# Expert tiles in pairs with the weights stationary, and another order of the work ahead of the experts

## The chip, the cores and the metric

The kernel runs on one core of one Trainium2 chip. The metric is the device time of one execution, from the runs' median. Engines are named PE (TensorE), ACT (ScalarE), DVE (VectorE), POOL (GpSimd) and SP (SyncE, which issues most of the DMA); each runs its own list of instructions in order, and they wait for one another through semaphores.

## The reference

The output is `x + attention(xn) + experts(xn)`, with `xn` the layer norm of `x` (2 x 1024 tokens of 512 values, fp32). Cut to what matters:

```python
# attention: 16 heads of 128 in 4 groups, causal, softmax, dense projection
# experts: sigmoid router with 8 groups of 4; the best 4 groups, then the best 6 of their experts
idx, w = _route(xf, Wr, br)                       # 6 of 32 experts for each of 2048 tokens
gate = zeros((T, E)).at[arange(T)[:, None], idx].add(w)
def step(acc, ew):
    w1, w2, g = ew                                # w1: 256 x 512, w2: 512 x 256
    h = square(relu(xf @ w1.T)) @ w2.T
    return (acc + g[:, None] * h, None)
shared = square(relu(x @ Ws1.T)) @ Ws2.T          # one shared expert, 512 wide
x + attn + shared + moe_out
```

## The kernel before

Every large product is made of three: an operand is split into an upper part that PE reads exactly (`_hi`, made by a copy on ACT) and the rest (`_lo`, subtracted on DVE), and hi x hi, hi x lo and lo x hi are summed in PSUM.

**Ahead of the experts.** 16 token tiles of 128 are loaded, normalised (`spread`, `normalize` on DVE, `root` on ACT, `normalize_last` on ACT), turned on PE (`turn_up`, 4 transposes), copied (`copy_up`), split (`upper_up`, `lower_up`) and multiplied with the router (`logits`, 8 fp32 products of 32 columns in the trace). The shared expert is 16 groups `hidden(j, m)` of 12 products of 512 columns, their relu, square and split on ACT and DVE (`relu_unit`, `square_unit`, `upper_unit`, `lower_unit`), and 16 groups `outputs(o, q)` of 12 products of 512 columns, added by DVE (`add_output`). From the logits DVE makes the routing, PE the ranks (`ranks`), and then DVE and ACT mark, token tile by token tile, which row of which expert's tile a token goes to (`mark_rows`: 6 `row_hot` of 128 columns, on ACT for odd tiles, and 6 `tile_hot` of MAXT columns), and PE sums the marks into a list of tokens (`list_rows`, 6 products of MAXT columns). `warm(n)` are products of ones that nobody reads. The order of all this on each engine is written out by hand, call by call.

**The experts.** An expert's tokens stand in tiles of 128 rows; `first_pair` holds where each expert's tiles begin, with at least 2 tiles for each. There are 111 tiles. POOL gathers the tokens of a tile by an indirect DMA into one of four slots (`xg`), four tiles ahead of PE. On PE a tile p is: `hidden_tile(p)`, 12 products of 256 columns with the tokens stationary (lines L861, L862, L865), in it the 4 transposes of the tokens of tile p+1 (L853); `output_tile(p-1)`, 6 products of 512 columns (L884, L885, L888); `transpose_hidden(p)`, 2 fp32 transposes (L897). In between ACT and DVE turn PSUM into operands: relu (L1242) on ACT, square (L1656) on DVE, transposed on PE, then `upper_hidden` (L1246, ACT) and `lower_hidden` (L1348, DVE); `upper_tokens` (L1231, ACT) and `lower_tokens` (DVE) do the same for the tokens; `copy_output` (L1252, ACT) takes the result of tile p-1 out of PSUM and SP stores it. ACT's order in a tile is relu(p), tokens(p+1), copy_output(p-1), upper_hidden(p).
An expert is its first tile, written out, and a loop over its others; four experts are written out in a loop of eight. Beside the first tile and behind the loop stand the four pieces of the weights of expert e+2: `upper_weights` (L1236, ACT, 512 columns) and `lower_weights` (DVE). They come by a 1 MB load of SP into one of two buffers (`eraw`), issued when the expert that had the buffer is lowered (`ew_lo`); the load for expert 2 (L472) waits for the four pieces of expert 0. The weights' slots alternate by pairs of experts between `wa_hi` and `w_hi`, so the names in the trace change every two experts.

**Behind them** comes attention, in eight groups, and the gathered sums of the experts' rows. `match_rows` reads what `y_filled` fills: the rows of `expert_outputs` above MINT tiles are filled with zeros by one DMA of ACT (L1180).

The named lines are those of the profile.

## Time and profile before

| | |
|---|---|
| median of 3 runs | 1529.18 us (1529.16 to 1531.23) |
| the profiled execution | 1530.99 us, its span 1529.2 us |
| mean granted clock of TensorE | 0.993 |
| PE, PEld, DVE, ACT, POOL busy | 99, 86, 74, 55, 19% of the span |
| chain of waits | PE 97%, DVE 2%, DMA 1% |
| ahead of the experts | 0 to 141.5 us |
| experts | 141.5 to 538.5 us |
| attention | 538.5 us to the end |

### The profile page before, as it was taken

To read this page: it belongs to the slowest core of one execution; us is meant where nothing else is said; L and a number is where in the kernel's file an instruction comes from. 1 tells how busy PE (TensorE), PEld (TensorE's weight loads), DVE (VectorE), ACT (ScalarE), POOL (GpSimd) and SP (SyncE) were. 2 spreads that over 40 slices of the span, in tenths; PEclk is the share of its full clock that TensorE was granted. 3 is DMA by queue.
4 is the path that set the end of the run, shared out by engine and by line. 5 is a ranking of instruction groups with operands and counts; after the bars stand their busy time and mean duration, and the time that the engine had idled before them with its cause. 6 is when DMAs were issued, how large, how long until landed. Compare 5 with 4: busy or idle time off the path is not lost.

```text
span 1529.2 us, 31143 instructions
## 1 busy us (share of the span) xinstructions
PE 1516.1 (99%) x8548; PEld 1308.5 (86%) x8549; DVE 1133.2 (74%) x2586; ACT 838.2 (55%) x1753; POOL 296.5 (19%) x540
## 2 busy tenths in 40 slices
PE   9999999999999999999999999999999999999998
PEld 7887888989888978888888888888888888888886
DVE  7887566666666669949948958966975994994896
ACT  5565666766766635535535634544553563553553
POOL 0002443444444301012002002102102101200211
PEclk8999999999999999999999999999999999999999
DMA  7875677777776712102102103412211210210111
GB/s 277 322 283 188 199 240 235 242 236 226 237 257 200 240 41 70 43 21 75 42 20 75 42 34 103 164 62 82 68 35 36 74 41 21 75 34 27 56 42 55
DMA packets 64774, 184.34 MB, mean 121 GB/s; under 512 B 7136, under 2 KB 7264, under 8 KB 60000
## 3 DMA queue, kind: packets, MB, share of 16 engines
q1 hardware_dynamic: 39888, 112.56, 20.9%
q0 software_dynamic: 16640, 54.54, 13.0%
q10 hardware_dynamic: 8208, 16.78, 2.8%
q8 instruction: 19, 0.31, 0.1%
q14 instruction: 19, 0.16, 0.0%
HBM read 123.29 MB, written 60.56 MB: 120 GB/s over the span
## 4 chain that ended last, share of the span: by engine, by line
PE 97%; DVE 2%; DMA 1%; ACT 0%; issue 0%; SPq 0%; DVEq 0%; ACTq 0%
PE bank L663 8%; PE bank L665 8%; PE bank L994 8%; PE bank L664 8%; PE ps_s L663 7%; PE ps_s L665 7%; PE ps_s L664 7%; PE ps_s L981 5%; PE ps_s L983 4%; PE ps_s L982 4%; PE ps_s L861 4%; PE ps_s L865 3%; PE ps_s L884 3%; PE ps_s L862 3%; PE ps_s L885 3%; PE ps_s L888 3%
## 5 line engine op out<-in xcount | busy, mean ns | idle before, releaser
L1323 ACT ACTIVATE probs<-probs,negmax 128x128 f32<-128x128 f32 (+7 forms) x256 | 197.4, 773 | 122.6 <-DVE negmax L1737 121.9
L1331 ACT ACTIVATE pT_hi<-bank 128x512 fp32r<-128x512 f32 x288 | 164.4, 595 | 143.6 <-PE bank L994 117.6
L1348 DVE TENSOR_TENSOR pT_lo<-bank,pT_hi 128x512 fp32r<-128x512 f32 x288 | 189.6, 684 | 41.1 <-ACT pT_hi L1331 40.1
L1737 DVE CUSTOM_DVE_ANT_0 probs<-ps_s,causal 128x128 f32<-128x128 f32 (+7 forms) x256 | 189.3, 752 | 17.2 <-PE ps_s L983 15.7
L427 POOL TENSOR_TENSOR settled<-ident 128x1 f32<-128x1 f32 x192 | 46.0, 239 | 789.0 <-DVE acc L1766 779.0
L994 PE MATMUL bank<-ident,probs 128*128 128x128 f32 x1152 | 157.0, 272 | 0.0
L994 PEld LDWEIGHTS bank<-ident,probs 128*128 128x128 f32 x1152 | 136.9, 141 | 19.8
L663 PE MATMUL ps_s<-xT_hi,wa_hi 128*128 128x512 f32 x384 | 152.7, 398 | 0.0
L665 PE MATMUL ps_s<-xT_hi,wa_lo 128*128 128x512 f32 x384 | 151.0, 393 | 0.0
L664 PE MATMUL ps_s<-xT_lo,wa_hi 128*128 128x512 f32 x384 | 150.3, 391 | 0.0
L1746 DVE TENSOR_SCALAR probs<-probs,rnorm 128x128 f32<-128x128 f32 (+7 forms) x256 | 133.4, 521 | 9.1
L981 PE MATMUL ps_s<-kT_hi,qT_hi 128*128 128x512 f32 (+5 forms) x384 | 134.0, 349 | 0.9 <-DVE qT_lo L1717 0.5
L983 PE MATMUL ps_s<-kT_hi,qT_lo 128*128 128x512 f32 (+5 forms) x384 | 131.2, 342 | 0.0
L982 PE MATMUL ps_s<-kT_lo,qT_hi 128*128 128x512 f32 (+5 forms) x384 | 130.9, 341 | 0.0
L663 PE MATMUL bank<-pT_hi,v_hi 128*128 128x512 f32 x288 | 123.6, 429 | 0.6 <-DVE cT_lo L1348 0.6
L1348 DVE TENSOR_TENSOR hT_lo<-ps_s,hT_hi 128x256 fp32r<-128x256 f32 x111 | 47.1, 424 | 93.6 <-ACT hT_hi L1246 91.9
L623 POOL DMA_INDIRECT xg<-normed_tokens,comb_idx x112 | 111.5, 995 | 24.0 <-issue 19.1
L665 PE MATMUL bank<-pT_hi,v_lo 128*128 128x512 f32 x288 | 113.5, 394 | 0.0
L1252 ACT ACTIVATE ysb<-ps_s 128x512 f32 x111 | 66.4, 598 | 85.6 <-PE ps_s L888 79.0
L664 PE MATMUL bank<-pT_lo,v_hi 128*128 128x512 f32 x288 | 112.7, 391 | 0.0
L652 POOL DMA_INDIRECT comb<-expert_outputs,comb_idx x96 | 105.1, 1095 | 19.7 <-issue 11.7
L663 PE MATMUL bank<-wa_hi,cT_hi 128*128 128x512 f32 x256 | 101.5, 396 | 1.4 <-DVE cT_lo L1348 1.4
(197 smaller groups left out, 3608.7 us busy)
## 6 DMA issues: line engine op xcount, KB each, us to landing
eraw<-we SPq DMA_DIRECT2D x37, 1024.0 KB, 7.4
expert_outputs<-ysb SPq DMA_DIRECT2D x111, 256.0 KB
araw<-wa SPq DMA_DIRECT2D x37, 512.0 KB, 3.8
expert_outputs<-comb ACTq DMA_DIRECT2D x1, 16384.0 KB, 44.2
normed_tokens<-xn SPq DMA_DIRECT2D x4, 1024.0 KB, 9.8
out<-acc SPq DMA_DIRECT2D x16, 256.0 KB, 2.6
acc<-x SPq DMA_DIRECT2D x2, 1024.0 KB, 13.7
turned_tokens<-xT_hi SPq DMA_DIRECT2D x2, 1024.0 KB, 6.3
```

The costliest lines, as they stand in the source:

```text
L663: pe.matmul(out_, lh, rh, start=(first and k == 0), stop=False)
L664: pe.matmul(out_, lh, rl, start=False, stop=False)
L665: mm = pe.matmul(out_, ll, rh, start=False, stop=(last and k == parts - 1))
L981: pe.matmul(o, q_h, kT_hi[:, ks], start=True, stop=False)
L982: pe.matmul(o, q_h, kT_lo[:, ks], start=False, stop=False)
L983: mm = pe.matmul(o, q_l, kT_hi[:, ks], start=False, stop=True)
L994: mm = pe.transpose(ps_t[blk % 2][:, h * P:(h + 1) * P], probs[:, i % 2, h, a * P:(a + 1) * P], ident[:, :])
L1323: act.activation(pr, pr, ACT.Exp, bias=negmax[:, i % 2, a:a + 1], scale=-1.0, accum_out=rowsum[:, i % 2, a:a + 1]).then_inc(exp_ready, 1)
L1331: act.activation(pT_hi[:, blk % RING, :], ps_t[blk % 2][:, :], ACT.Copy).then_inc(pt_hi_ready, 1)
L1348: dve.tensor_tensor(out_, whole, upper.bitcast(F32), ALU.subtract).then_inc(signal, 1)
L1737: dve.tensor_tensor_reduce(halves(probs[:, i % 2, a, 0:keys]), ps_s[:, s:s + parts, 0:keys // parts], halves(causal[:, SQ - keys:]), -1.0, ...
L1746: dve.tensor_scalar(pr, pr, rnorm[:, i % 2, a:a + 1], None, ALU.mult).then_inc(probs_ready, 1)
```

## The change

Five things change.

1. The first two tiles of every expert are a pair. Their tokens lie side by side (`xgT_hi`, `xgT_lo` get a dimension of 2), the weights are the stationary operand and the two tiles' 256 tokens the moving one (`hidden_pair`). The result is already turned, so there is no `transpose_hidden` for the two; ACT and DVE work on 128 x 256 for each m (`relu_pair`, `upper_pair` with Square on ACT, `square_pair`, `lower_pair` on DVE). `output_first` gives the first tile's result in a bank of its own (`ps_y2`), `output_tile` the second's in the turn behind.
2. An expert on PE is now `turn_tokens(lo+1)`, `output_tile(lo-1)` of the expert before, `hidden_pair`, `turn_tokens(lo+2)`, `output_first`, and the loop from the third tile on. `turn_tokens(q, bank)` is the choice of the slot and the 4 transposes that `hidden_tile` had inside.
3. The weight pieces stand in other places: 0 and 1 ahead of the pair's relu, 2 between m=0 and m=1, 3 behind `copy_output(lo)`.
4. Every expert has at least LEAST = 3 tiles, and MAXT follows a formula: 177 in place of 160.
5. The order written out ahead of the experts is another one on PE, ACT and DVE, with WARM 18 instead of 12. Up to the experts' loop the calls are the same but for one `warm(2)` fewer between the first logits. `lower_unit(6, 1)`, `add_output(2, 2)` and `add_output(2, 3)` move behind the copy of the list, and DVE waits for `room_free` before the first attention scores.

The core of the diff, the orders cut to what the prediction speaks of:

```diff
-MAXT = MINT + 2 * E
+LEAST = 3
+MAXT = max(LEAST * (E - n) + min(n * TILES, (T * TOPK + (P - 1) * n) // P) for n in range(E + 1))
...
-WARM = 12
+WARM = 18
...
             turn_up(0, 0)
+            warm(2)
             turn_up(0, 1)
-            warm(2)
             logits(0, 0)
-            warm(2)
             turn_up(0, 2)
+            logits(0, 1)
             turn_up(0, 3)
             warm(6)
-            logits(0, 1)
+            logits(0, 2)
             warm(2)
-            logits(0, 2)
             turn_up(0, 4)
             logits(0, 3)
             turn_up(0, 5)
+            turn_up(0, 6)
             logits(0, 4)
-            turn_up(0, 6)
             logits(0, 5)
             turn_up(0, 7)
+            hidden(0, 0)
             logits(0, 6)
-            hidden(0, 0)
             hidden(0, 1)
+            turn_up(1, 0)
+            logits(0, 7)
+            turn_up(1, 1)
             hidden(1, 0)
-            logits(0, 7)
-            turn_up(1, 0)
             hidden(1, 1)
-            turn_up(1, 1)
...
-            turn_up(1, 5)
-            logits(1, 2)
+            logits(1, 3)
             turn_up(1, 6)
             turn_up(1, 7)
-            logits(1, 3)
             logits(1, 4)
             logits(1, 5)
             logits(1, 6)
             logits(1, 7)
+            hidden(4, 0)
             outputs(0, 0)
+            hidden(4, 1)
             outputs(0, 1)
-            hidden(4, 0)
+            hidden(5, 0)
+            ranks()
+            hidden(5, 1)
             outputs(0, 2)
             outputs(0, 3)
-            ranks()
-            hidden(4, 1)
+            hidden(6, 0)
+            list_rows(0)
+            hidden(6, 1)
+            list_rows(1)
...
             outputs(2, 2)
-            list_rows(13)
-            outputs(2, 3)
             list_rows(14)
             list_rows(15)
+            outputs(2, 3)
             outputs(3, 0)
             outputs(3, 1)
             outputs(3, 2)
...
+        ps_x2 = banks[0][:, :]
+        ps_p = [bank[:, 0:2 * P] for bank in banks[1::2]]
+        ps_y2 = banks[2][:, :]
...
+            def hidden_pair(lo, s):
+
+                w_hi, w_lo = w1(hi_slot(s)), w1(lo_slot(s))
+                both = lambda x, k: x[:, k, :, :].rearrange("p t n -> p (t n)")
+                for m in range(KM):
+                    ms = slice(m * P, (m + 1) * P)
+                    if m == 0:
+                        pe.wait_ge(mx_hi, lo + 2)
+                    for k in range(KD):
+                        pe.matmul(ps_p[m], w_hi[:, k, ms], both(xgT_hi, k), start=(k == 0), stop=False)
+                        pe.matmul(ps_p[m], w_lo[:, k, ms], both(xgT_hi, k), start=False, stop=False)
+                    if m == 0:
+                        pe.wait_ge(mx_lo, lo + 2)
+                    for k in range(KD):
+                        mm = pe.matmul(ps_p[m], w_hi[:, k, ms], both(xgT_lo, k), start=False, stop=(k == KD - 1))
+                    mm.then_inc(mh_ready, 1)
+
+            def output_first(lo, s):
+
+                w_hi, w_lo = w2(hi_slot(s)), w2(lo_slot(s))
+                for m in range(KM):
+                    pe.wait_ge(mhhi_ready, past(lo + (m + 1)))
+                    pe.matmul(ps_y2, hT_hi[:, m, 0, :], w_hi[:, m, :], start=(m == 0), stop=False)
+                    pe.matmul(ps_y2, hT_hi[:, m, 0, :], w_lo[:, m, :], start=False, stop=False)
+                    pe.wait_ge(mhlo_ready, past(lo + (m + 1)))
+                    mm = pe.matmul(ps_y2, hT_lo[:, m, 0, :], w_hi[:, m, :], start=False, stop=(m == KM - 1))
+                mm.then_inc(my_ready, 1)
...
             def expert_tiles(e, s, lo, hi, es):
 
-                pe.wait_ge(ew_lo, (e + NSH) * WP + 2)
-                hidden_tile(lo, slot_of(s))
-                after = pair_bound(pe, e + 2)
+                turn_tokens(lo + 1, ps_x2)
                 if s:
                     output_tile(lo - 1, slot_of(s - 1))
                 else:
                     with pe.If(es > 0):
                         output_tile(lo - 1, slot_of(SLOTS - 1))
-                transpose_hidden(lo, (e + (NSH + 1)) * WP)
-                with pe.Fori(lo + 1, hi) as p:
+                after = pair_bound(pe, e + 2)
+                pe.wait_ge(ew_lo, (e + NSH) * WP + 2)
+                hidden_pair(lo, slot_of(s))
+                pe.sem_inc(mt_ready, 2)
+                turn_tokens(lo + 2, ps_x)
+                pe.wait_ge(ew_lo, (e + (NSH + 1)) * WP)
+                output_first(lo, slot_of(s))
+                with pe.Fori(lo + 2, hi) as p:
                     hidden_tile(p, slot_of(s))
                     output_tile(p - 1, slot_of(s))
                     transpose_hidden(p)
...
+            def relu_pair(lo, m):
+
+                act.wait_ge(mh_ready, lo + (m + 1))
+                act.wait_ge(mhsq_ready, past(lo))
+                act.activation(prelu[:, m, :], ps_p[m], ACT.Relu).then_inc(mrelu_ready, 1)
+
+            def upper_pair(lo, m):
+
+                act.wait_ge(mrelu_ready, past(lo + (m + 1)))
+                act.activation(hT_hi[:, m, :, :].rearrange("p t n -> p (t n)"), prelu[:, m, :],
+                               ACT.Square).then_inc(mhhi_ready, 1)
+
...
             def expert_uppers(e, s, lo, hi, es):
 
                 arrived, slot = e // 2 + (NSH // 2 + 2), slot_of(s + 2)
-                relu_hidden(lo)
-                upper_tokens(lo + 1)
+                upper_tokens(lo + 1, 1)
                 upper_weights(0, slot, arrived)
                 if s:
                     copy_output(lo - 1)
                 else:
                     with act.If(es > 0):
                         copy_output(lo - 1)
-                upper_hidden(lo)
                 after = pair_bound(act, e + 2)
                 upper_weights(1, slot, arrived)
-                with act.Fori(lo + 1, hi) as p:
+                relu_pair(lo, 0)
+                upper_pair(lo, 0)
+                upper_weights(2, slot, arrived)
+                relu_pair(lo, 1)
+                upper_pair(lo, 1)
+                upper_tokens(lo + 2)
+                copy_output(lo, ps_y2)
+                upper_weights(3, slot, arrived)
+                with act.Fori(lo + 2, hi) as p:
                     relu_hidden(p)
                     upper_tokens(p + 1)
                     copy_output(p - 1)
                     upper_hidden(p)
-                upper_weights(2, slot, arrived)
-                upper_weights(3, slot, arrived)
...
+            def square_pair(lo, m):
+
+                dve.wait_ge(mrelu_ready, past(lo + (m + 1)))
+                dve.tensor_tensor(phsq[:, m, :], prelu[:, m, :], prelu[:, m, :], ALU.mult).then_inc(mhsq_ready, 1)
+
+            def lower_pair(lo, m):
+
+                dve.wait_ge(mhhi_ready, past(lo + (m + 1)))
+                dve.wait_ge(mhsq_ready, past(lo + (m + 1)))
+                subtract(hT_lo[:, m, :, :].rearrange("p t n -> p (t n)"), phsq[:, m, :],
+                         hT_hi[:, m, :, :].rearrange("p t n -> p (t n)"), mhlo_ready)
...
             spread(0)
+            spread(1)
             normalize(0)
-            spread(1)
             normalize(1)
             spread(2)
             lower_up(0, 0)
+            lower_up(0, 1)
             normalize(2)
-            lower_up(0, 1)
             lower_up(0, 2)
             lower_shared(0, 0, 1)
+            lower_up(0, 3)
             lower_shared(0, 1, 2)
+            spread(3)
...
             dve.wait_ge(started, 4)
+            lower_unit(6, 1)
+            add_output(2, 2)
+            add_output(2, 3)
             lower_unit(7, 0)
             lower_unit(7, 1)
-            add_output(2, 3)
+            lower_weights(0, 0, slot_of(0))
+            lower_weights(0, 1, slot_of(0))
             add_output(3, 0)
-            lower_weights(0, 0, slot_of(0))
             add_output(3, 1)
+            lower_weights(0, 2, slot_of(0))
             add_output(3, 2)
-            lower_weights(0, 1, slot_of(0))
-            lower_weights(0, 2, slot_of(0))
-            lower_weights(0, 3, slot_of(0))
             lower_tokens(0)
             add_output(3, 3)
+            lower_weights(0, 3, slot_of(0))
             for c in range(WP):
                 lower_weights(1, c, slot_of(1))
...
             def expert_lowers(e, s, lo, hi, es):
                 slot = slot_of(s + 2)
-                square_hidden(lo)
-                lower_tokens(lo + 1)
+                lower_tokens(lo + 1, 1)
                 lower_weights(e + 2, 0, slot)
-                lower_hidden(lo)
                 after = pair_bound(dve, e + 2)
                 lower_weights(e + 2, 1, slot)
-                with dve.Fori(lo + 1, hi) as p:
+                square_pair(lo, 0)
+                lower_pair(lo, 0)
+                lower_weights(e + 2, 2, slot)
+                square_pair(lo, 1)
+                lower_pair(lo, 1)
+                lower_tokens(lo + 2)
+                lower_weights(e + 2, 3, slot)
+                with dve.Fori(lo + 2, hi) as p:
                     square_hidden(p)
                     lower_tokens(p + 1)
                     lower_hidden(p)
-                lower_weights(e + 2, 2, slot)
-                lower_weights(e + 2, 3, slot)
```

## Rows read from the trace of the kernel before

**Rows 1.** Busy time by stage: stretch; busy us of each engine; PEclk; DMA share; GB/s.
```profile
17.00:27.00 10.00, 10.00 (x44) 9.42 (x43) 9.85 (x27) 3.96 (x8) 0.00 (x0) 0.50 1.04 390
58.00:65.00 7.00, 7.00 (x23) 5.89 (x23) 4.60 (x11) 3.61 (x7) 0.00 (x0) 0.52 1.00 402
146.00:150.00 4.00, 4.00 (x19) 3.61 (x19) 2.74 (x5) 2.39 (x5) 0.94 (x4) 0.59 1.00 406
175.13:535.70 360.57, 360.57 (x2449) 323.81 (x2448) 225.36 (x426) 245.06 (x528) 144.55 (x297) 1.00 0.73 233
```

**Rows 2.** Timeline, start of the kernel: start us, us, engine, line, what, [idle before].
```profile
14.96 1.92 DVE L1398 TENSOR_SCALAR xn<-res,mv,rstd 128x512 f32<-128x512 f32 x4
...
24.16 0.77 PE L663 MATMUL ps_s<-xT_hi,w_hi 128*128 128x512 f32 x1
...
33.91 0.97 PE L700 MATMUL bank<-wr_sb,xf 128*128 128x32 f32 x8
```

**Rows 3.** Timeline of PE, an expert of three tiles, its last tile in parts.
```profile
256.74 0.36 PE L861 MATMUL ps_s<-wa_hi,xgT_hi 128*128 128x256 f32 x1
...
263.89 0.36 PE L861 MATMUL ps_s<-wa_hi,xgT_hi 128*128 128x256 f32 x1
...
265.41 0.60 PE L853 MATMUL ps_s<-ident,xg 128*128 128x128 f32 x4
265.77 0.48 PE L884 MATMUL ps_s<-wa_hi,hT_hi 128*128 128x512 f32 x1
...
267.24 0.38 PE L897 MATMUL ps_s<-ident,mhsq 128*128 128x128 f32 x2
267.38 0.36 PE L861 MATMUL ps_s<-w_hi,xgT_hi 128*128 128x256 f32 x1
```

**Rows 4.** Timeline of PE, end of the last tile of the last expert.
```profile
535.70 0.38 PE L897 MATMUL ps_s<-ident,mhsq 128*128 128x128 f32 x2
536.96 0.50 PE L884 MATMUL ps_s<-w_hi,hT_hi 128*128 128x512 f32 x1 [0.88 <-ACT hT_hi L1246]
...
538.46 0.40 PE L663 MATMUL ps_s<-xT_hi,wa_hi 128*128 128x512 f32 x1
```

**Rows 5.** Timeline of ACT, the same place.
```profile
536.03 0.60 ACT L1252 ACTIVATE ysb<-ps_s 128x512 f32 x1 [0.93 <-PE ps_s L888]
536.53 0.38 ACT L1246 ACTIVATE hT_hi<-ps_s 128x256 fp32r<-128x256 f32 x1
```

**Rows 6.** Timeline of all engines, from the end of a hidden product group to the square.
```profile
194.65 0.60 PE L853 MATMUL ps_s<-ident,xg 128*128 128x128 f32 x4
194.85 0.38 ACT L1242 ACTIVATE mrelu<-ps_s 128x256 f32<-128x256 f32 x1 [0.64 <-PE ps_s L865]
...
195.27 0.43 DVE L1656 TENSOR_TENSOR mhsq<-mrelu 128x256 f32<-128x256 f32 x1 [0.59 <-ACT mrelu L1242]
```

**Rows 7.** Timelines of SP, PE, DVE and ACT, the first expert.
```profile
141.01 0.33 SPq L472 DMA_DIRECT2D eraw<-we  x1
...
141.47 0.28 PE L861 MATMUL ps_s<-wa_hi,xgT_hi 128*128 128x256 f32 x1
...
142.28 2.49 DVE L1348 TENSOR_TENSOR wa_lo<-eraw,wa_hi 128x512 fp32r<-128x512 f32 x4
...
145.16 0.44 PE L897 MATMUL ps_s<-ident,mhsq 128*128 128x128 f32 x2 [1.67 <-DVE mhsq L1656]
...
145.89 0.63 ACT L1236 ACTIVATE w_hi<-eraw 128x512 fp32r<-128x512 f32 x1 [1.77 <-DMA eraw<-we]
...
157.36 0.38 PE L897 MATMUL ps_s<-ident,mhsq 128*128 128x128 f32 x2
```

**Rows 8.** Timelines of PE and DVE, the ranks and the marks.
```profile
78.17 2.22 PE L751 MATMUL bank<-rsel,ones 128*128 128x480 f32 x15
...
94.92 1.07 DVE L1525 TENSOR_SCALAR row_hot<-lane,xf 128x128 f16<-128x128 f16 x6 [2.63 <-PE bank L761]
...
125.86 1.46 DVE L1527 TENSOR_SCALAR tile_hot<-lane,xf,tok_f 128x160 f16<-128x160 f16 x6
```

More of the change, by code:

```diff
@@ L883, in output_tile, with transpose_hidden @@
                 for m in range(KM):
-                    pe.matmul(ps_y, hT_hi[:, m, :], w_hi[:, m, :], start=(m == 0), stop=False)
-                    pe.matmul(ps_y, hT_hi[:, m, :], w_lo[:, m, :], start=False, stop=False)
+                    pe.matmul(ps_y, hT_hi[:, m, 1, :], w_hi[:, m, :], start=(m == 0), stop=False)
+                    pe.matmul(ps_y, hT_hi[:, m, 1, :], w_lo[:, m, :], start=False, stop=False)
                 pe.wait_ge(mhlo_ready, past(p + 1))
                 for m in range(KM):
-                    mm = pe.matmul(ps_y, hT_lo[:, m, :], w_hi[:, m, :], start=False, stop=(m == KM - 1))
+                    mm = pe.matmul(ps_y, hT_lo[:, m, 1, :], w_hi[:, m, :], start=False, stop=(m == KM - 1))
                 mm.then_inc(my_ready, 1)
-            def transpose_hidden(p, weights=None):
+            def transpose_hidden(p):
                 pe.wait_ge(mhsq_ready, past(p + 1))
                 for m in range(KM):
-                    if m and weights is not None:
-                        pe.wait_ge(ew_lo, weights)
                     mm = pe.transpose(ps_g[:, m * P:(m + 1) * P], mhsq[:, m * P:(m + 1) * P], ident[:, :])
@@ L1143, in _ @@
             square_unit(0, 0)
             relu_unit(0, 1)
+            copy_up(1, 0)
+            upper_up(0, 7)
             upper_unit(0, 0)
-            root(4)
+            relu_unit(1, 0)
+            copy_up(1, 1)
+            relu_unit(1, 1)
+            exponent(0)
+            upper_up(1, 0)
+            copy_up(1, 2)
+            upper_up(1, 1)
+            copy_up(1, 3)
+            upper_up(1, 2)
+            normalize_last()
             square_unit(0, 1)
+            relu_unit(2, 0)
@@ L1646, in _, with lower_tokens @@
             dve.wait_ge(hot_used, TILES)
             dve.tensor_copy(tok_idx[:, 0:MAXT], ps_list).then_inc(list_ready, 1)
-            def lower_tokens(q):
+            def lower_tokens(q, second=0):
                 dve.wait_ge(mx_hi, q + 1)
-                subtract(xgT_lo[:, :, :], ps_x.rearrange("p (k n) -> p k n", k=KD), xgT_hi[:, :, :], mx_lo)
+                subtract(xgT_lo[:, :, second, :], (ps_x, ps_x2)[second].rearrange("p (k n) -> p k n", k=KD),
+                         xgT_hi[:, :, second, :], mx_lo)
@@ L1731, in attend_dve @@
                             dve.wait_ge(pt_ready, n * TRI + blocks_before(i - 1))
+                        if isinstance(n, int) and n == 0 and unit == 0:
+                            dve.wait_ge(room_free, 1)
                         s = 2 * (unit % 2)
```

279 lines of the change are left out of this document (132 added, 147 removed).

## The prediction

> **What bounds the kernel now.** I read the chain of waits first: nearly all of it is PE. Then busy time by stage: in the expert stage PE is busy for all of 360.57 us, at the full granted clock [rows 1]. So only time on PE's own line counts, or a wait that opens in it. Ahead of the experts PE is also back to back from 16 us on, but two stretches run at the lower of its two levels (1.2 instead of 2.4 GHz): 17 to 27 us and 58 to 65 us [rows 1]. Each has fp32 logits and transposes ahead of it; the first shared-expert product starts at 24.16 [rows 2]. The attention stage behind the experts (538.46 on) is the same in both kernels but for one wait, dealt with below.
>
> **Steady expert tile.** In the timeline of PE a tile is: 12 products of 256 columns, 263.89 to 265.41 (1.52 us); 4 transposes of the next tokens to 265.77 (0.36); 6 products of 512 columns to 267.24 (1.47); 2 transposes of the hidden values to 267.38 (0.14); in all 3.49. The four products at 264.93 take 0.48, so 12 of them are 1.43, and the 0.09 over that is a slow restart behind fp32 transposes. An expert of three tiles takes 10.64 (256.74 to 267.38, where the weights' name changes) [rows 3]. There are 111 tiles; by the changes of name and the tile starts no expert has fewer than three, so the new least of 3 (it was 2) pads nothing.
>
> **The pair: what goes.** hidden_pair has the same 24 products of 256 columns as two tiles had: 24 x 0.119 = 2.85 us. What goes is transpose_hidden for both, with the slow restart behind it, 2 x (0.14 + 0.09) = 0.46, and the 0.15 by which an expert's first tile is now longer than its others (10.64 - 3 x 3.49). Saved per expert: 0.6 us, 19 us over 31 experts, if no wait opens.
>
> **The pair: the wait that it opens.** Now a tile's hidden transposes are followed by the next tile's 12 products and 4 transposes (1.87 us), and these cover the trip over ACT before output_tile. In the change an expert begins with turn_tokens(lo+1) and then at once output_tile(lo-1). The trace shows this trip without cover once, behind the last tile: transposes at 535.70, the output products at 536.96, with 0.88 us idle [rows 4]. ACT's rows say why: the copy of the output before it starts at 536.03, and only behind it, at 536.53, hT_hi [rows 5]. That order stays. Of the 1.26 us the transposes (0.13) and turn_tokens (0.35 + 0.05 of restart) cover 0.53, so each of 31 seams has a new PE wait of 0.73 us.
> The rest of such an expert, from T, the start of the last hidden transposes: output_tile from T+1.26, 1.50 long (536.96 to 538.46) to 2.76; the pair to 5.61; turn_tokens(lo+2) to 5.96; output_first. Its last product wants mhlo for m=1: PE's end at 5.61 + 0.20 to ACT's relu (194.65 to 194.85), + 0.42 to DVE (195.27) [rows 6] = 6.23; but DVE first lowers weight piece 2 (0.60 each: four of them from 142.28, 2.49 with the tail of the last [rows 7]), whose upper half, 0.63 long behind relu and Square of m=0, leaves ACT at 5.7, so the square starts near 6.3, the subtract at 6.8 and PE has it at 7.3; it wants it at 7.21. Wait: 0.1. Then output_first ends at 7.53, hidden_tile 1.43 to 8.96, turn 0.35, output_tile 1.47: the next T is at 10.78. Against 10.64 that is **+0.14 us for an expert of three tiles**, and the same for those of four and five, since a tile of the inner loop stays 3.49. 31 x 0.14 = +4.3. Bounds for one expert: -0.6 (the trip fully covered) to +0.5 (PE's register load, which now stands between output_tile and the pair with little queued ahead of it, costs up to 0.4; now it has backlog and no row shows it). I take +0.14, since both of its ends are rows of the same operations. The sem_inc of mt_ready is an instruction of PE's queue alone and hides in the products' backlog. ACT's and DVE's other work is the same but for the copies and squares of 2 x 256 columns; the weight loads of DMA are asked for at T+3.6 of the expert before, about 8.7 us ahead of use, and one took 4.9.
> The gathers of POOL keep four slots and four tiles of lead. The wait of DVE on room_free before the first attention scores costs nothing: the last store goes out near 540 and the scores come 8 projections of 2.8 us later.
>
> **The first expert.** The load for expert 2 is issued when lower_weights(0,3) is done, now 141.01, and lands for ACT at 145.89, 4.9 later [rows 7]. PE ends the stage before at E = 141.47. In the change lower_weights(0,3) stands behind add_output(3,3), which waits for PE's end: done at E+1.5, landed at E+6.4. And ACT has upper_weights(0) of that load ahead of relu_pair(0), so the relu starts at E+7.5 and output_first at E+8.4 (relu 0.42, square and subtract 0.42 each, as in [rows 6]), where PE stood ready at E+6.8, having waited 2.4 us before that for mx_lo behind four lower_weights on DVE (E+4.5). The first two tiles are done at E+10.75, two more take 6.7 to the last hidden transposes: E+17.5. With one more stretch at the lower clock behind these gaps (+1.0 on what is not waiting) E+18.5, against E+15.9 before (157.36) [rows 7]: **+2.6**, bounds 0 and +5.
>
> **The other order ahead of the experts.** spread(1) before normalize(0) puts the first transposes 1.3 later; 18 warm products instead of 12 fill just that. Tokens 4 to 7 are normalised at 14.2 instead of 14.96 [rows 2]: 0.75 earlier. logits(0,6) goes behind hidden(0,0), out of the slow stretch: twice 0.81 there, 0.81 at the full clock (33.91 to 34.72) [rows 2]. With PE's last gap before these transposes gone too, hidden(0,0) starts at 21.1 instead of 24.16, about 2.3 of it real. In the second slow stretch ten us of nothing but logits and transposes preceded the outputs; now two of the eight logits, two turns and two products stand apart and some 5 us are left in a row, so I take the stretch of 7 us, worth 3.4, as gone. Ranks end at 74.7 instead of 80.25 (78.17 + 2.1) [rows 8]: -5.5. From there to E are 61.2 us now. In them DVE's marks pace the lists: it waits 2.6 us for PE once (94.92), which the new order, with lists put in earlier, spares; but MAXT goes from 160 to 177, and six tile_hot take 1.46 with the tail of the last, 0.23 each [rows 8], so 96 of them with 17 columns more cost between 0 and 96 x 0.025 = 2.4, and I take 1.7. The last list then comes 6.4 earlier than now, and behind it PE has one output group more than it has now, 2.9, and half a us of restarts. So E = 74.7 + 61.2 - 2.6 + 1.7 + 3.4 = 138.4: **-3.1**, bounds -6.5 (DVE never late) and 0 (the second slow stretch stays, 3.4 less the 0.3 above). The fill of expert_outputs grows from 16.8 to 21.2 MB, from 44 to 56 us; it ends near 115, ahead of its first reader.
>
> **The sum.** -3.1 + 2.6 + 4.3 = +3.8 us. The profiled execution took 1530.99 (span 1529.22 and 1.8 around it), so 1534.8 on its scale; the median of the runs is 1.8 lower, 1529.18, so **1533.0**. From no change a measurement can tell about 0.2%, 3.06 us: the limits are 1526.1 and 1532.2.
>
> **Clock between the gaps.** Behind the last tile 0.88 us idle did not lower the clock: the six products of 512 columns behind it take 1.50 [rows 4], as at full clock (1.47 in [rows 3]). At the first expert 1.67 us of idle up to 145.16 [rows 7] was followed by a lower clock: 0.59 in the mean from 146 to 150 [rows 1], 3.4 us at the lower level. The Trainium skill, page "TensorE: Matmul & The Clock Gate", section "A second HAM failure mode: psum-queue depth-cycling", tells of short idles between groups of products that recur often enough for the clock to swing between its levels. That speaks against this change, which makes 31 such idles; by the one row at hand they are too short.
>
> **The rivals.**
> 1. The seam is covered and the pair pays: 31 x -0.64 = -19.8, with -3.1 and +2.6: -20.3, 1508.9. For it: PE's work itself is 10.0 us for three tiles. Against it: [rows 4, 5]. This is the case on the other side; it decides as soon as hT_hi is ready less than 0.5 us behind the transposes.
> 2. Nothing net: the seam costs what the transposes gave (0 per expert) and the first expert's wait is half of mine: -3.1 + 1.3 = -1.8, 1527.4. For it: +0.14 is the difference of two sums of 10 us.
> 3. The recurring gaps lower the clock, once per expert 3.4 us at half speed: 31 x 1.7 = +53, 1586. For it: it happened after 145. Against: [rows 4].
> 4. The order ahead brings nothing, since the slow stretch stays or DVE's marks come late: +2.6 + 4.3 = +6.9, 1536.1.
>
> **How the numbers follow.** Forecast 0.48, rival 1 0.13, rival 2 0.18, rival 3 0.06, rival 4 0.15. The forecast's own range is 1529 to 1540; about 0.15 of its 0.48 is under 1532.2. Faster: rival 1 and 0.07 of rival 2, 0.20. Same: 0.15 of the forecast, 0.11 of rival 2 and 0.01 of rival 4, 0.27. Slower: 0.53. The range of 8 in 10 leaves out rivals 1 and 3 and reaches down to half a covered seam (31 x 0.35 less, 1521) and up to 0.4 more in a third of the experts on top of rival 4: 1520 to 1543.
>
> **What would show it.** PE idle before the output products (now L884) with ACT's hT_hi as releaser, 31 times, 0.7 us; three-tile experts of 10.8; first expert 18.5 us from the last shared output to the transposes of its last tile; the first shared-expert product at 21; full clock at 58 to 65; the last list near 123; the shared stage's end near 138. I am wrong if the three-tile expert is 10.3 or less, if the granted clock in the expert stage is below 1.00, or if the stage ahead ends behind 141.

## The result, and the profile after

The changed kernel takes 1540.99 us (median of 4 runs, 1539.26 to 1541.67) against 1529.20 (4 runs, 1529.16 to 1531.23): 1.0086 times as long, 95% interval 1.0063 to 1.0109. By the medians it is slower by 11.8 us, where 3.8 were predicted. The profiled execution took 1539.26 us, its span is 1537.5.

Three marks on PE's timeline cut each span into four parts: up to E, the start of the next tokens' transposes or products behind the last shared output; the first expert, from E to T, the start of its last hidden transposes; the other 31 experts, to the T of the last; and the rest. A seam is the place where one expert's last tile meets the next expert's first. Each ratio is to runs of before that were taken with the experiment (medians 1530.87 for e1 to e4, 1530.44 for e5 to e8, 1530.38 for e9 to e12), so it differs a little from a quotient with 1529.20.

| kernel | median us (runs) | ratio to before, 95% interval | E | first expert | 31 experts | rest of the span |
|---|---|---|---|---|---|---|
| before | 1529.20 (4) | | 141.47 | 15.89 | 378.34 | 993.5 |
| changed | 1540.99 (4) | 1.0086 (1.0063 to 1.0109) | 134.34 | 18.85 | 393.56 | 990.8 |
| e1 order alone | 1525.43 (12) | 0.9976 (0.9959 to 0.9993) | 134.45 | 16.61 | 378.46 | 993.1 |
| e2 pair alone | 1543.93 (5) | 1.0103 (1.0069 to 1.0137) | 142.01 | 16.22 | 393.64 | 990.3 |
| e3 piece 2 later | 1532.37 (12) | 1.0023 (1.0004 to 1.0041) | 134.56 | 18.92 | 386.75 | 990.3 |
| e4 seam | 1534.06 (12) | 1.0041 (1.0022 to 1.0060) | 135.64 | 19.23 | 387.12 | 990.3 |
| e5 160 columns | 1542.77 (4) | 1.0076 (1.0062 to 1.0091) | 135.57 | 19.10 | 393.54 | 993.4 |
| e6 before, 18 warm | 1529.42 (12) | 0.9988 (0.9972 to 1.0003) | 139.92 | 14.51 | 377.83 | 993.1 |
| e7 both mends | 1521.60 (5) | 0.9941 (0.9928 to 0.9954) | 137.71 | 17.54 | 376.27 | 990.1 |
| e8 and first expert | 1518.29 (5) | 0.9925 (0.9911 to 0.9938) | 134.71 | 15.70 | 376.29 | 989.8 |
| e9 changed, 12 warm | 1540.52 (6) | 1.0096 (1.0061 to 1.0131) | 136.10 | 18.18 | 393.75 | 990.5 |
| e10 layout | 1518.12 (8) | 0.9936 (0.9911 to 0.9960) | 134.01 | 15.79 | 376.12 | 990.1 |
| e11 wide | 1526.21 (10) | 0.9979 (0.9960 to 0.9997) | 136.75 | 15.75 | 376.17 | 996.0 |
| e12 old order, mends | 1525.60 (12) | 0.9966 (0.9948 to 0.9985) | 142.25 | 15.39 | 376.29 | 990.1 |

For the change: -7.1 + 3.0 + 15.2 - 2.7 = +8.3 us of span. The other 3.5 us of the 11.8 are scatter: the profiled execution of before is 1.8 above its median, that of the changed kernel 1.7 below, and before's 29 runs beside e1 to e4 went from 1521.0 to 1534.1.

Busy time by stage, of the changed kernel (the columns of [rows 1]: stretch; us, PE, PEld, DVE, ACT, POOL; PEclk; DMA share; GB/s):
```profile
17.00:27.00 10.00, 10.00 (x68) 8.92 (x67) 9.54 (x24) 5.48 (x11) 0.00 (x0) 1.00 1.04 396
58.00:65.00 7.00, 7.00 (x32) 5.68 (x31) 6.40 (x64) 1.12 (x2) 0.00 (x0) 1.00 1.00 371
140.00:147.00 7.00, 6.38 (x24) 4.99 (x24) 4.11 (x8) 4.24 (x10) 1.91 (x3) 0.51 0.94 372
153.19:546.75 393.56, 382.28 (x2445) 323.16 (x2444) 234.45 (x446) 269.70 (x552) 157.15 (x312) 1.00 0.70 224
```
Both slow stretches ahead of the experts are gone, where [rows 1] had 0.50 and 0.52, and the first one behind E is longer. In the 31 experts PE, never idle in [rows 1], is idle for 11.3 us, 5.4 of them ahead of the seams' output products, 4.9 ahead of the transposes of tokens that an expert now begins with, and 0.9 inside output_first; the clock stays at 1.00.

The timeline of PE, one expert of three tiles (start us, duration, line, what; to be held against [rows 3]):
```profile
304.07 0.38 PE L930 MATMUL ps_s<-ident,mhsq 128*128 128x128 f32 x2
304.48 0.65 PE L858 MATMUL bank<-ident,xg 128*128 128x128 f32 x4
305.33 0.50 PE L920 MATMUL ps_s<-wa_hi,hT_hi 128*128 128x512 f32 x1 [0.21 <-issue]
...
306.84 0.28 PE L883 MATMUL bank<-xgT_hi,wa_hi 128*128 128x256 f32 x1
...
309.72 0.60 PE L858 MATMUL ps_s<-ident,xg 128*128 128x128 f32 x4
310.08 0.48 PE L896 MATMUL bank<-wa_hi,hT_hi 128*128 128x512 f32 x1
...
311.59 0.51 PE L899 MATMUL bank<-wa_hi,hT_lo 128*128 128x512 f32 x1
311.93 0.28 PE L907 MATMUL ps_s<-wa_hi,xgT_hi 128*128 128x256 f32 x1
...
315.20 0.38 PE L930 MATMUL ps_s<-ident,mhsq 128*128 128x128 f32 x2
```
The expert takes 11.13. From the hidden transposes to the output product are 1.26, as at the tail of [rows 4]; the mean over 31 seams is 1.28. The profile puts this wait down to hT_hi at some seams and to no releaser ("issue") at others; here ACT's hT_hi ends at 305.28, 0.05 ahead of the product. The pair takes 2.88. The six products of output_first, 310.08 to 311.93, take 1.85, where 1.57 was predicted.

ACT, then DVE, beside that output_first:
```profile
307.84 0.63 ACT L1274 ACTIVATE w_hi<-eraw 128x512 fp32r<-128x512 f32 x1
...
309.22 0.62 ACT L1274 ACTIVATE w_hi<-eraw 128x512 fp32r<-128x512 f32 x1
309.92 0.39 ACT L1286 ACTIVATE prelu<-bank 128x256 f32<-128x256 f32 x1
```
```profile
308.50 0.69 DVE L1402 TENSOR_TENSOR w_lo<-eraw,w_hi 128x512 fp32r<-128x512 f32 x1 [1.41 <-ACT w_hi L1274]
309.11 0.42 DVE L1709 TENSOR_TENSOR phsq<-prelu 128x256 f32<-128x256 f32 x1
309.63 0.43 DVE L1402 TENSOR_TENSOR hT_lo<-phsq,hT_hi 128x256 fp32r<-128x256 f32 x1
309.98 0.69 DVE L1402 TENSOR_TENSOR w_lo<-eraw,w_hi 128x512 fp32r<-128x512 f32 x1
310.58 0.42 DVE L1709 TENSOR_TENSOR phsq<-prelu 128x256 f32<-128x256 f32 x1
311.10 0.43 DVE L1402 TENSOR_TENSOR hT_lo<-phsq,hT_hi 128x256 fp32r<-128x256 f32 x1
```
DVE waits last at 308.50. From there to the second hT_lo it goes from one operation to the next, weight piece 2 (309.98) among them, and PE's last product starts 0.49 behind the start of that hT_lo.

The first expert, to be held against [rows 7], and the tail:
```profile
134.34 0.60 PE L858 MATMUL bank<-ident,xg 128*128 128x128 f32 x4
135.62 0.39 PE L883 MATMUL bank<-xgT_hi,wa_hi 128*128 128x256 f32 x1 [0.69 <-ACT xgT_hi L1268]
...
138.89 0.74 PE L888 MATMUL bank<-xgT_lo,wa_hi 128*128 128x256 f32 x4 [2.05 <-DVE xgT_lo L1402]
...
143.12 0.76 PE L896 MATMUL bank<-wa_hi,hT_hi 128*128 128x512 f32 x1 [0.62 <-DVE w_lo L1402]
...
153.19 0.38 PE L930 MATMUL ps_s<-ident,mhsq 128*128 128x128 f32 x2
...
546.75 0.38 PE L930 MATMUL ps_s<-ident,mhsq 128*128 128x128 f32 x2
548.01 0.50 PE L920 MATMUL ps_s<-w_hi,hT_hi 128*128 128x512 f32 x1 [0.89 <-ACT hT_hi L1296]
```
Three waits of PE stand behind E; the tail's wait is that of [rows 4].

### The profile page after: what moved, and what is told of

It is laid out like the page before. It is cut to its first block, busy times and chain, and to the rows that moved or that the text cites. A ratio compares the mean times of both kernels' runs of the same rounds, so it can differ in the third digit from the quotient of the medians.

```text
span 1537.5 us, 30805 instructions
## 1 busy us (share of the span) xinstructions
PE 1512.3 (98%) x8424; PEld 1286.4 (84%) x8425; DVE 1132.4 (74%) x2586; ACT 851.2 (55%) x1753; POOL 302.6 (20%) x540
## 4 chain that ended last, share of the span: by engine, by line
PE 84%; issue 7%; DVE 5%; ACT 1%; POOL 1%; ACTq 1%; DMA 1%; DVEq 0%; POOLq 0%; SPq 0%
PE bank L669 7%; PE bank L1031 7%; PE bank L671 7%; PE bank L670 7%; PE ps_s L669 6%; PE ps_s L671 6%; PE ps_s L670 6%; PE ps_s L1018 4%; PE ps_s L1020 4%; PE ps_s L1019 4%; PE ps_s L920 3%; PE ps_s L924 2%; PE ps_s L921 2%; PE ps_s L858 2%; PE ps_s L911 1%
## 5 line engine op out<-in xcount | busy, mean ns | idle before, releaser
L433 POOL TENSOR_TENSOR settled<-ident 128x1 f32<-128x1 f32 x192 | 49.3, 257 | 786.5 <-DVE acc L1839 776.5
L629 POOL DMA_INDIRECT xg<-normed_tokens,comb_idx x112 | 117.5, 1049 | 23.8 <-issue 18.6
L671 PE MATMUL bank<-wa_hi,cT_lo 128*128 128x512 f32 x256 | 100.0, 391 | 0.0
L670 PE MATMUL bank<-wa_lo,cT_hi 128*128 128x512 f32 x256 | 99.7, 390 | 0.0
```

The lines of the kernel that those rows point to most:

```text
L670: pe.matmul(out_, lh, rl, start=False, stop=False)
L671: mm = pe.matmul(out_, ll, rh, start=False, stop=(last and k == parts - 1))
```

## The experiments

**e1: the order ahead of the experts and 18 warm products, in the kernel before.** The four blocks of PE, ACT and DVE are the changed kernel's; the experts are the old ones.

> The kernel before with one part of the change: the order ahead of the experts on PE, ACT and DVE and 18 warm products; the experts, their least of 2 and the 160 columns of the lists as before. Theory A (the traces of before and after are the sum of three terms: order -7.1, first expert +3.0, seams 31 x 0.49 = +15.2): the stage ahead ends near 134.3, and the old first expert is late only by the load that is now asked for behind it, 0 to +1.5: 1522.1 to 1523.6. Theory B (the order was sized right in the prediction, -3.1, and 4 us of the gap between the profiles is chance): 1526 to 1527.5. Theory C (an earlier end only makes the first expert wait for its weights, and all is given back there): 1528 to 1530.

Measured 0.9976, -3.7 us (-6.3 to -1.1); the medians differ by 5.4. E is 134.45, the first expert takes 0.7 longer than before, the rest is as before. Theory A by the trace. But the runs say more. With the mean granted clock at 1.000 the kernel before takes 1521.0 and 1521.7 us, at 0.997 1524.2, at 0.992 and 0.993 (15 of 29 runs) 1530.9 and more; the order alone takes 1523.8 to 1527.9 at 1.000 to 0.996. So its gain is a clock that stays up, and at the same clock it is some 2.5 us slower. Most of that is the first expert: 16.61 at a clock of 1.00 here, with 2.26 us of idle ahead of its first hidden transposes, against 14.51 at 1.00 and 1.67 in e6, which has the old order. The windows of e1:
```profile
17.00:27.00 10.00, 10.00 (x68) 8.93 (x66) 9.25 (x23) 5.74 (x12) 0.00 (x0) 1.00 1.04 392
58.00:65.00 7.00, 7.00 (x32) 5.68 (x31) 6.41 (x62) 1.12 (x2) 0.00 (x0) 1.00 0.98 348
```

**e2: the pair alone.** The changed kernel with the old order and 12 warm products.

> The changed kernel with the old order ahead of the experts and 12 warm products: the pair alone, with lists of 177 columns. Theory A: +15.2 from the seams and 0 to +3 from the first expert (the load for expert 2 is asked for ahead of the last output group again, so that part of its delay goes; the four lowerings of weights ahead of the first pair's marks stay): +15 to +18, 1544 to 1547. Theory B (the pair costs +4.3 + 2.6 as predicted and the rest of the +11.8 lies in how the new order and the pair meet): 1535 to 1537.

Measured 1.0103, +15.8 us (+10.6 to +21.0): theory A. The 31 experts take 393.64, as in the changed kernel, so nothing in them comes from the order. The first expert loses only 0.3 (at a clock of 0.89 in both; at 1.00 it is 15.39 in e12 against 14.51 in e6, 0.9). So most of its 3.0 in the changed kernel is the two parts' meeting.

**e3: weight piece 2 later**, on ACT and DVE:
```
-    lower_weights(e + 2, 2, slot)
     square_pair(lo, 1)
     lower_pair(lo, 1)
     lower_tokens(lo + 2)
+    lower_weights(e + 2, 2, slot)
```

> The changed kernel with weight piece 2 cast on ACT and lowered on DVE behind the next tokens instead of ahead of the second half of the pair. Theory A (output_first is late by 0.37 because DVE runs back to back from weight piece 1 to the lower part of hidden half 1): output_first falls from 1.84 to 1.5 and the kernel gains up to 31 x 0.35 = 11 us, 1530; less whatever the next tokens or the output copy now wait for. Theory B (output_first is late by the round trip of the second half itself, 0.2 + 0.42 + 0.42 + 0.42 behind its last product): the gain is under 31 x 0.1 = 3 us, 1538 to 1541. Rival: the weights come too late and tile 2 waits: slower than 1541.

Measured 1.0023 against the changed kernel's 1.0086: 9.6 us by the ratios, 8.6 by the medians, 6.8 of them in the 31 experts. Output_first fell from 1.83 to 1.61 in the mean of 30. Theory A in kind; 0.22 per expert, not 0.35, since two waits of 0.2 stay, for the second half's hT_hi and for its hT_lo. What PE's weight loads waited for (us in total, times, longest), the changed kernel from 160 to 540, then e3 from 160 to 520:
```profile
PEld bank L899 <- DVE hT_lo L1402: 13.8, 30, 0.5
PEld bank L896 <- ACT hT_hi L1291: 6.7, 30, 0.2
```
```profile
PEld bank L899 <- DVE hT_lo L1402: 7.0, 29, 0.2
PEld bank L896 <- ACT hT_hi L1291: 6.6, 29, 0.2
```
The wait for the second half's hT_lo falls from 0.46 to 0.24 each time; the one for its hT_hi stays at 0.2.

**e4: the seam.** The last output_tile of an expert goes to the other bank, and in ACT's loop
```
-    copy_output(p - 1)
     upper_hidden(p)
+    copy_output(p - 1)
```
with a wait for that copy ahead of the inner tiles' output products.

> The changed kernel with the last output_tile of an expert written to the other output bank, so that ACT can do upper_hidden of a tile ahead of the copy of the output before it. Theory A (the trip of 1.29 at the seam is ACT's copy of 0.5 plus upper_hidden): the seam's wait falls from 0.77 to between 0.3 and 0.5, 31 x 0.3 = 9 us and the same at the tail once, 1532; inner tiles stay at 3.48. Theory B (the seam is bound by PE's own sequencer, the loop's exit and the turn's start, and the copy hides behind it): 0 to 3 us, 1538 to 1541. Rival: the later copy makes output_first or DVE's store wait, and what the seam gains is given back there: 1541.

Measured 1.0041, 6.9 us less than the changed kernel, 6.4 in the 31 experts. The trip from hidden transposes to output product fell from 1.28 to 0.98, and at the tail from 1.26 to 0.85. But output_first grew to 1.97. PE and ACT at one seam:
```profile
303.21 0.38 PE L932 MATMUL ps_s<-ident,mhsq 128*128 128x128 f32 x2
303.63 0.65 PE L858 MATMUL bank<-ident,xg 128*128 128x128 f32 x4
304.06 0.49 PE L922 MATMUL bank<-wa_hi,hT_hi 128*128 128x512 f32 x1
```
```profile
303.63 0.39 ACT L1298 ACTIVATE hT_hi<-ps_s 128x256 fp32r<-128x256 f32 x1 [1.01 <-issue]
303.91 0.59 ACT L1304 ACTIVATE ysb<-ps_s 128x512 f32 x1
```
The upper half is now first on ACT, and the turn of tokens (0.43) covers what is left of it. Theory A; 0.3 x 31, some 9.5 us, gained, 0.14 x 31 = 4.3 given back in output_first, and 0.02 less in each of output_tile and the pair. At 24 of the 31 seams the trip is now 0.85 to 0.96; at the other seven it is 1.21 to 1.44, of which more in e7.

**e5: lists and buffer of 160 columns**, MAXT = MINT + 2 * E.

> The changed kernel with lists of 160 columns instead of 177 (MAXT = MINT + 2 E), so that the buffer of expert outputs and its fill are as large as before; nothing else. Theory A (17 more columns cost nothing behind the new order, since the marks are ahead of PE, and the attention stage is 2.7 us shorter in all kernels with the pair for another reason, such as where the loop's code lies): 1540 to 1541 and 990.3 us from the last hidden transposes to the end. Theory B (the larger buffer is what changed the attention stage, 990.3 us instead of 993.3): it is back at 993.3, 1543. Theory C (DVE's marks paced the stage ahead as the prediction had it, 1.7 us): 1539 and a stage that ends near 132.7.

Measured 1.0076, not to be told from 1.0086. E and the experts don't move beyond scatter, but the rest of the span is back at 993.4: theory B, or something that goes with the width (e10).

**e6: the kernel before with 18 warm products.**

> The kernel before with 18 warm products instead of 12; nothing else. The runs of before on the last chip went from 1521.0 at a mean granted clock of 1.000 to 1534.1 at 0.992, those of the order alone from 1523.8 (1.000) to 1527.9 (0.996). Theory A (the order's gain is the clock: the new order with 18 products keeps PE at full clock from the start, and at the same clock the old order is 2 to 3 us faster): if the 6 products alone hold the clock, 1522 to 1524 with little scatter, faster than the order alone. Theory B (it is the logits apart from one another that hold it, and the 6 products do nothing): 1530 with the scatter of before, from 1521 to 1534. Theory C (the work itself is shorter in the new order, as the prediction had it): 1529 to 1532 at a clock near 0.998.

Measured 0.9988 (0.9972 to 1.0003), runs from 1521.1 (clock 0.999) to 1532.4 (0.992): theory B. Its first stretch is slow again, the second partly:
```profile
17.00:27.00 10.00, 10.00 (x46) 9.23 (x46) 9.85 (x27) 4.07 (x8) 0.00 (x0) 0.55 1.04 392
58.00:65.00 7.00, 7.00 (x30) 5.82 (x30) 5.46 (x12) 3.61 (x7) 0.00 (x0) 0.76 1.01 402
```

**e7: both mends, e3 and e4.**

> The changed kernel with both mends at once: weight piece 2 behind the next tokens, and the seam's output product in the other bank with upper_hidden ahead of the copy. Alone they took 7.3 and 5.9 us off the profiled span. In the second, output_first grew from 1.83 to 1.97 and gave back 4 us of it. Theory A (that stall was DVE's queue up to the lower part of half 1, which the first mend empties): the gains add and more, output_first 1.6 to 1.7, an expert of three tiles 10.4 to 10.5: span 1516 to 1518, 1518 to 1520. Theory B (output_first in the second mend waits for the other bank's copy, not for DVE): output_first stays near 1.9 and the kernel at 1525 to 1527.

Measured 0.9941 (0.9928 to 0.9954), faster than before. The 31 experts take 376.27: 17.3 less than in the changed kernel, where the mends alone took 6.8 and 6.4. Output_first is 1.61 and the seam 0.98, so e4's loss there was DVE's queue; an expert of three tiles takes 10.45. Theory A; the profiled span was 1521.6, not 1516 to 1518, as E came 3 us later in this execution. What is left, at PE's weight loads from 160 to 520:
```profile
PEld bank L858 <- issue: 10.2, 24, 0.9
PEld bank L899 <- DVE hT_lo L1404: 7.2, 30, 0.2
PEld bank L896 <- ACT hT_hi L1293: 6.7, 30, 0.2
```
The first line is the turn of tokens behind the tile loop's exit; the changed kernel has it too, with the same numbers in the same window. Where the outer loop over four experts also turns round, the turn starts 0.78 to 1.04 behind the start of the hidden transposes (seven seams), at the others 0.22 to 0.56, and the output product follows 0.4 to 0.6 later. No run changed the loops, so that their exits are the cause is argued from where these seven stand, not shown.

**e8: the first expert as well.**
```
-    add_output(3, 3)
     lower_weights(0, 3, slot_of(0))
     for c in range(WP):
         lower_weights(1, c, slot_of(1))
+    add_output(3, 3)
```

> The kernel with both mends, and DVE's last addition ahead of the experts moved behind its five lowerings of weights, so that the load for expert 2 is asked for 2.0 us earlier and xgT_lo comes 0.8 earlier. Theory A (the first expert's 18.9 us are that load and the marks of its second tile): first expert 17 instead of 18.9, 1516 to 1518. Theory B (the lower clock behind the gaps and ACT's casts ahead of relu set it): under 0.5 gained, as both mends, 1518 to 1520.

Measured 0.9925 (0.9911 to 0.9938), 1518.29 us. The first expert takes 15.70; the load for expert 2 is issued at 134.13 instead of 135.91:
```profile
134.71 0.60 PE L858 MATMUL bank<-ident,xg 128*128 128x128 f32 x4
136.00 0.39 PE L883 MATMUL bank<-xgT_hi,wa_hi 128*128 128x256 f32 x1 [0.69 <-ACT xgT_hi L1270]
137.71 0.74 PE L888 MATMUL bank<-xgT_lo,wa_hi 128*128 128x256 f32 x4 [0.49 <-DVE xgT_lo L1404]
...
141.64 0.47 PE L896 MATMUL bank<-wa_hi,hT_hi 128*128 128x512 f32 x1 [1.31 <-DVE w_lo L1404]
```
```profile
134.71:150.41 15.70, 13.09 (x85) 11.01 (x84) 10.18 (x19) 8.29 (x18) 5.78 (x12) 1.00 0.78 292
```
Theory A, and more than its 17. The wait for xgT_lo fell from 2.05 to 0.49, that for w_lo rose from 0.62 to 1.31, so 0.9 of the 3.15 us by which the changed kernel's first expert is longer is idle. Most of the rest is the clock: 1.00 here, 0.82 in the mean over the changed kernel's 18.85 us. That the shorter idle kept it up is likely, not shown: the three kernels with an idle of 0.49 have 1.00, the six with one of 2.05 have 0.82 to 0.91, but e1 has an idle of 2.26 there and 1.00, and e2 and e12, with the same idles of 0.69 and 1.45, have 0.89 and 1.00.

**e9: the changed kernel with 12 warm products.**

> The changed kernel with 12 warm products instead of 18. 18 of them did nothing for the order of before (0.9988, interval 0.9972 to 1.0003, with the same scatter from 1521 to 1532). Theory A (it is the new order's place for the fp32 logits and transposes that holds the clock, not the warm products): mean clock 0.997 to 0.998 and 1540 to 1541 with little scatter. Theory B (both are needed): clock 0.993 to 0.995 in most runs, 1544 to 1547.

Measured 1.0096 (1.0061 to 1.0131). Four of six runs took 1539.4 to 1540.5 at a clock of 0.996 to 0.998, as theory A has it; the other two 1550.1 and 1551.0 at 0.989 and 0.991, which neither expected. So with 12 products the new order held the clock in four runs of six, and that the six more add nothing is not shown. The profiled run, one of the four, speaks for some effect: its clock is 0.86 from 5 to 17 us, where the changed kernel has 1.00, and its E is 1.8 later.

**e10 and e11: the width of one row of on-chip memory.** Both are e8, with in e10 lists of 160 columns again and
```
-    tok_idx = sb("tok_idx", [P, MAXT + 1], I32)
+    tok_idx = sb("tok_idx", [P, MAXT + 18], I32)
```
and in e11 177 columns and `[P, 192]`.

> The kernel with both mends and the first expert mended, with lists and a buffer of 160 columns again, and the on-chip row of token lists kept 178 columns wide, so that all that lies behind it in on-chip memory keeps the changed kernel's addresses. Theory A (the attention stage is 993.3 us in all four kernels with 160 columns and 990.2 in all six with 177 because of the addresses on the chip): 990, 1518 in all. Theory B (it is the size of the buffer in the device's memory, from which the combination gathers, or its fill): 993, 1521.

> The kernel with both mends and the first expert mended, with the row of token lists 192 columns wide instead of 178 (768 bytes instead of 712), which moves all that lies behind it by 56 bytes and nothing else. Theory A (addresses on the chip set the attention stage's pace, and a multiple of 64 bytes is the best place): 990 or less, down to 987. Theory B (the size of the buffer in the device's memory sets it): 990 unchanged, 1518.

e10 measured 0.9936, rest of the span 990.1: with 160 columns in the buffer and the addresses of 177, theory A. e11 measured 0.9979, rest 996.0: addresses again, but the wrong way for the guess on 64 bytes. The page's groups of projection products, e10 and then e11:
```profile
L669 PE MATMUL ps_s<-xT_hi,wa_hi 128*128 128x512 f32 x384 | 151.3, 394 | 0.0
L671 PE MATMUL ps_s<-xT_hi,wa_lo 128*128 128x512 f32 x384 | 150.2, 391 | 0.0
L670 PE MATMUL ps_s<-xT_lo,wa_hi 128*128 128x512 f32 x384 | 149.7, 390 | 0.0
```
```profile
L669 PE MATMUL ps_s<-xT_hi,wa_hi 128*128 128x512 f32 x384 | 153.0, 398 | 0.0
L671 PE MATMUL ps_s<-xT_hi,wa_lo 128*128 128x512 f32 x384 | 151.9, 396 | 0.0
L670 PE MATMUL ps_s<-xT_lo,wa_hi 128*128 128x512 f32 x384 | 151.8, 395 | 0.0
```

**e12: both mends with the order of before.**

> The kernel with both mends (without the edit of the first expert's lowerings, which this order has ahead already), with the order of before ahead of the experts and 12 warm products. Theory A (the new order's gain is the clock alone, and at full clock the old order is 2 to 3 us faster): scatter of 10 us or more, from 1516 at a clock of 1.000 to 1527 at 0.992, median 1524 to 1526. Theory B (the new order is shorter in work too): no run under 1520.

Measured 0.9966 (0.9948 to 0.9985), from 1518.0 at a clock of 0.999 to 1528.3 at 0.993, median 1525.6: theory A. E is 142.25. At a clock of 0.999 the same mends took 1521.6 with the new order (e7) and 1518.0 with the old, and the first expert is 17.54 there and 15.39 here; e8's edit makes up for that. Here too the old order's best run (1518.0) is no slower than e8's (1518.15), and its median is 7.3 above.

## Why the prediction was right or wrong

**Direction and range: right, and partly by luck.** 1541.0 is inside 1520 to 1543, but above the forecast's own 1529 to 1540. The sum was off by 8.0 us. Of these 4.5 are in the profiled spans (8.3 for 3.8): +10.9 in the experts, -4.0 in the order ahead, +0.4 in the first expert and -2.7 in the rest of the span, so two large terms were missized and partly cancelled. The other 3.5 are scatter. With the experts' term alone as measured the forecast would have been near 1544, outside the range.

**The seam: right.** Predicted 1.26 from the hidden transposes to the output product, measured 1.28 in the mean. e4 shows the cause that was named: ACT's copy ahead of hT_hi. The idle was to be 0.7 at each seam; the profile shows 10.3 us over the 31, 0.33 each, as it draws every transpose out to the end of its pipeline. The start times carry the argument.

**The second wait, "Wait: 0.1": this step failed.** Output_first was to end at T+7.53 and ends at T+7.86 (304.07 to 311.93). The prediction started the square of half 1 at T+6.3 and had the last product at T+7.3; they came at 6.51 and 7.52. It had counted ACT's cast of piece 2 and DVE's lowering, but not that DVE already runs late from weight piece 1 (308.50) through square and lower half to piece 2, with no wait that the profile shows. The cast left ACT at T+5.77, where 5.7 was predicted; DVE took it up at T+5.91, so of the 0.21 by which the square came late 0.07 are ACT's and 0.14 DVE's queue. e3 moves piece 2 on both engines and takes 0.22 out; it doesn't part the two. e7 takes out with it what e4 had pushed into the same queue. Output_first is 0.28 over the prediction here; with 0.05 more in pair and turn and 0.02 behind it this makes 11.13 - 10.78 = 0.35 per expert, 10.9 us in all.
The bound of +0.5 rested on a register load of PE ahead of the pair that could cost 0.4, for which no row of before was given. In the changed kernel the pair's first product starts 0.22 to 0.30 behind the one before it, so it costs next to nothing. The 0.15 by which an expert's first tile was longer is 0.17 by the prediction's own rows, which changes nothing.

**The first expert: right, 2.96 for 2.6,** and by its mechanism: xgT_lo came at E+4.55 for 4.5, the load at E+6.43 for 6.4. e8 takes most of it out with the order of DVE's queue alone, e2 shows that the old order hardly has it. The clock's part was put at +1.0 and is larger: the first experts of the changed kernel and of before ran at 0.82 and 0.89, which over 18.85 and 15.89 us is some 3.4 and 1.7 us of lost time. And the clock does not follow from the idle as the prediction had it. The kernel before and e6 have the same first expert and the same 1.67 us of idle in it (the columns of [rows 1], the clock third from the end):
```profile
141.47:157.36 15.89, 14.22 (x89) 12.77 (x88) 9.79 (x19) 7.26 (x16) 5.65 (x13) 0.89 0.76 280
139.92:154.43 14.51, 12.84 (x89) 11.43 (x88) 9.70 (x19) 7.17 (x16) 5.83 (x13) 1.00 0.84 307
```
So e8's 15.70 at full clock is still 1.2 us longer than the old first expert at full clock.

**The order ahead: -7.1 for -3.1, beyond the bound of -6.5.** Both slow stretches went, as predicted for the second and half for the first. The first shared product starts at 19.32, not 21.1, and at full clock; the ranks end at 71.75 instead of 74.7, and from there to E are 62.6 us instead of 63.7. DVE's later marks and the 17 columns, put at +1.7, cost nothing that shows (e5). One reading was wrong in kind: the prediction took the slow stretches of [rows 1] for a property of the old order, and they are there in some runs only. By e1 and e12 the order's worth is that of the clock, on average, and at full clock it brings nothing. The rows bear this out: at 0.50 over 10 us, 0.52 over 7 and 0.89 over 15.89 the clock took 5.0 + 3.4 + 1.7 = 10.1 us from the profiled execution of before, by estimate, and 1531.0 - 10.1 = 1520.9 is its quickest runs' time (1521.0 and 1521.7 at a clock of 1.000). No trace shows a quick run of before, so this is worked out and not seen. What decides in a given run whether the clock falls stays open.

**The rest of the span,** taken as equal, is 2.7 us shorter, through 68 bytes of layout.

**The rivals.** The covered seam was priced at -19.8; with both mends the pair is worth 376.27 - 378.34 = -2.1, since the trip is still 0.98 where 0.53 is covered, and output_first is 1.61 instead of 1.48: 0.45 + 0.13 = 0.58 of the 0.64 hoped for. Without the seven late seams the trip would be 0.87, still 0.34 too long. The recurring gaps did not lower the clock: 1.00 over 393.56 us with 31 seams and 11.3 us of idle, none longer than 0.7. The rule of the Trainium skill, page "TensorE: Matmul & The Clock Gate", section "A second HAM failure mode: psum-queue depth-cycling", is not borne out by idles of this size.

The best of these kernels is e8 (e10 is the same within their intervals): 0.9925 of before. Against the changed kernel it is 0.984 by the ratios (0.9925 / 1.0086) and 0.985 by the medians.

## What to carry to other kernels

When a change takes work off the busiest engine, replay the queue of every engine that feeds it, operation by operation, from the last place where that engine waits: a 0.6 us piece of another expert's weights, which nobody waited for yet, cost 7 us here by standing ahead of an operand that PE did wait for, and two mends of 6.8 and 6.4 us were worth 17.3 together. Before crediting an order with a gain, look at the granted clock of several runs. A profile of a kernel whose time scatters by 13 us with its clock is one draw. And keep the addresses fixed when comparing: hold the total width of small tables constant.

## What the runs showed of the hardware that was not expected

The width of a small table moved the attention stage by 6 us, with no idle ahead of the products that slowed down. The table is that of the token lists, `tok_idx`. Rows of 161 words gave 993.1 to 993.5 us in four kernels, 178 words 989.8 to 990.8 in nine, 192 words 996.0 in one. The mean step of the 1152 projection products, from start to start with jumps over 0.45 us left out, is 0.2294 or 0.2295 us in four kernels with 178 words (changed, e8, e10, e12), 0.2312 to 0.2314 in the four with 161, and 0.2343 in e11; from e10 to e11 that is 1152 x 0.0048 = 5.5 of the 5.9 us. Which array's address it is, and against what it must stand, is open.

Where an expert ends, PE's next work starts 0.22 to 0.56 us behind the start of the two hidden transposes, and 0.78 to 1.04 where the outer loop turns too (e7). PE is idle for 0 to 0.18 of the first and 0.40 to 0.66 of the second. That it is the loops' exits, with nothing queued behind them, is the likely reading; no run varied them.

Equal work with equal idles ran at different clocks: the old first expert, with 1.67 us of idle, at 0.89 in the kernel before and at 1.00 in e6, and the pair's behind the old order, with 0.69 and 1.45, at 0.89 in e2 and 1.00 in e12.
